# Graph attention on one core: the addition of x goes from VectorE to GpSimd

## What is computed

```python
h = jnp.maximum(_layernorm(x, axis=-1), 0.0)
# inside _L0_gnn_ref, with h as its x
    h = jnp.einsum('ni,hif->hnf', x, W)
    s1 = jnp.einsum('hnf,hf->hn', h, a1)
    s2 = jnp.einsum('hnf,hf->hn', h, a2)
    scores = jax.nn.leaky_relu(s1[:, :, None] + s2[:, None, :], negative_slope=0.2)
    scores = jnp.where(adj[None] > 0, scores, NEG_BIG)
    att = jax.nn.softmax(scores, axis=-1)
    out = jnp.einsum('hnm,hmf->hnf', att, h)
    return jax.nn.elu(out)          # heads side by side, 512 wide
x = x + _L0_gnn_ref(h, adj, W, a1, a2)
```

## Time and profile before

| what | value |
|---|---|
| median of three runs | 812.9 us |
| the profiled execution's own time | 814.42 us |
| its span in the trace | 812.6 us |
| mean granted TensorE clock | 0.864 |
| DVE busy | 687.4 us, 85% of the span |
| PE busy | 610.1 us, 75% |
| ACT busy | 471.6 us, 58% |
| POOL busy | 388.6 us, 48% |

### The profile page before, as it was taken

One profiled execution on the slowest core, in us unless ns is written; L12 is line 12 of the kernel. 1 busy time (PEld: TensorE's weight loads), 2 busy tenths in 40 slices (PEclk: granted clock), 3 DMA queues, 4 the chain that ended last, 5 costly groups with the idle time before them and its releaser, 6 DMA issues.

```text
span 812.6 us, 9242 instructions
## 1 busy us (share of the span) xinstructions
PE 610.1 (75%) x2182; PEld 357.3 (44%) x2182; DVE 687.4 (85%) x2066; ACT 471.6 (58%) x695; POOL 388.6 (48%) x775
## 2 busy tenths in 40 slices
PE   0698988897688758553886697768878859988874
PEld 0364554454354434342543354444444435554442
DVE  4897998997777677564999799999999988999995
ACT  0647999989999989225565365647453213233322
POOL 4644544442333332227776336447375655757610
PEclk9998999989998997855999698886887869999997
DMA  9956999999999999328999999999996766969852
GB/s 289 424 207 229 339 411 417 417 403 407 422 421 419 420 421 423 150 66 316 407 409 417 406 367 400 413 414 397 410 398 199 263 194 204 297 206 296 288 174 105
DMA packets 65130, 269.51 MB, mean 332 GB/s; under 512 B 12145, under 2 KB 12145, under 8 KB 52786
## 3 DMA queue, kind: packets, MB, share of 16 engines
q1 hardware_dynamic: 45314, 203.12, 63.1%
q0 software_dynamic: 19760, 65.78, 23.6%
HBM read 243.49 MB, written 25.37 MB: 331 GB/s over the span
## 4 chain that ended last, share of the span: by engine, by line
DVE 26%; PE 12%; issue 8%; DMA 6%; POOL 3%; ACT 0%; DVEq 0%; POOLq 0%
DVE nodes L1098 8%; PE psO L1237 7%; DMA nodes<-table,list_column 4%; DVE places L248 4%; PE psO L1243 3%; DVE best L237 3%; DVE agg L1109 2%; DMA nodes<-table,column 2%; POOL nodes L934 2%; DVE to_row L1068 1%; DVE result L1121 1%; POOL nodes L929 1%; PE psC L1223 1%; DVE owner L1032 1%; PE psD L1238 1%
## 5 line engine op out<-in xcount | busy, mean ns | idle before, releaser
L601 PE MATMUL psH<-sb_W,normedT 128*128 128x512 f32 x384 | 225.5, 678 | 0.0
L1237 PE MATMUL psO<-nodes,ident 128*128 128x512 f32 x276 | 183.7, 758 | 43.5 <-issue 39.9
L227 ACT ACTIVATE packed<-adj_rows,eight 128x3072 uint8<-128x3072 int32 x66 | 188.3, 2853 | 0.7
L929 POOL DMA_INDIRECT nodes<-table,column x138 | 135.3, 980 | 85.5 <-PE psD L1244 45.0
L934 POOL DMA_INDIRECT nodes<-table,list_column x109 | 112.5, 1032 | 86.9 <-DVE list_column L1057 56.4
L1098 DVE TENSOR_TENSOR nodes<-nodes,psW 128x2048 f32<-128x2048 f32 (+4 forms) x66 | 138.7, 2142 | 0.0
L1243 PE MATMUL psO<-nodes,to_row 128*128 128x512 f32 x218 | 124.9, 661 | 6.3 <-DVE nodes L1098 6.1
L643 POOL TENSOR_TENSOR sb_node_sum<-sb_node_sum,h_rows 128x512 f32<-128x512 f32 x48 | 61.2, 1275 | 141.6 <-ACT h_rows L566 141.6
L602 PEld LDWEIGHTS psS<-sb_Wa,normedT 128*128 128x128 f32 x384 | 78.6, 205 | 103.5 <-issue 103.5
L248 DVE FIND_INDEX8 places<-best,packed 128x8 uint32<-128x96 f32 (+6 forms) x240 | 109.9, 465 | 0.0
L237 DVE MAX8 best<-packed 128x8 f32<-128x96 f32 (+6 forms) x240 | 102.8, 460 | 0.5 <-ACT packed L227 0.5
(11 more groups left out here) (177 smaller groups left out, 923.3 us busy)
## 6 DMA issues: line engine op xcount, KB each, us to landing
adj_rows<-in_adj_dram SPq DMA_DIRECT2D x66, 1536.0 KB, 10.7
sb_adj_rows<-in_adj_dram SPq DMA_DIRECT2D x30, 1536.0 KB, 14.6
table<-h_rows SPq DMA_DIRECT2D x48, 260.0 KB, 9.0
sb_x_rows<-in_x_dram SPq DMA_DIRECT2D x48, 256.0 KB, 9.2
kept<-in_x_dram SPq DMA_DIRECT2D x19, 512.0 KB, 7.0
out_dram<-result SPq DMA_DIRECT2D x19, 512.0 KB, 4.0
kept<-in_x_dram SPq DMA_DIRECT2D x10, 256.0 KB, 8.8
out_dram<-result SPq DMA_DIRECT2D x10, 256.0 KB, 7.6
```

Source lines behind the costliest of these rows:

```text
L227: nc.scalar.activation(words.bitcast(mybir.dt.uint8), sb["adj_rows"][buffer_of(i)][:], ACT.Square, bias=sb["eight"][:], scale=-17.0, accum ...
L601: nc.tensor.matmul(psH[:, t % 2], normedT[:, t % 2, kc], sb["W"][:, kc], start=(kc == 0), stop=(kc == KC - 1))
L929: nc.gpsimd.indirect_dma_start(out=nodes[:, node_at[u] + i * w.direct + j], out_offset=None, in_=table, in_offset=bass.IndirectOffsetOnAxi ...
L1237: nc.tensor.matmul(psO[:, o, to], sb["ident"][:], nodes[:, n0 + q, 0:HF], start=a, stop=False)
```

## The change

The kernel before computes kept = max(agg, 0) + x on DVE in `normalise`, and result = (exp(min(agg, 0)) - 1) + kept on DVE in `finish`. The kernel after leaves the first away and computes result = max(exp(min(agg, 0)) - 1, agg) on DVE in `finish`, which is elu(agg), and then result = result + x on POOL, in place, in a new function `add_x`. POOL does this for the group of unit u-4 after it has issued all gathers of unit u, that is two units later than `finish` stands on DVE. The store and the next load of x, which SP issues, wait for POOL's addition.

```diff
+            def add_x(g):
+
+                w, o = GROUPED[g], g % 2
+                pool.wait_ge(bent, g + 1)
+                pool.wait_ge(x_loaded[o], 16 * (g // 2 + 1))
+                nc.gpsimd.tensor_tensor(result[:, o, 0:w.tiles], result[:, o, 0:w.tiles], kept[:, o, 0:w.tiles], ALU.add).then_inc(finished, 1)
             for u, w in enumerate(UNITS):
...
                                                  ).then_inc(gathered[k], 16)
+                if u >= 4 and UNITS[u - 4].last:
+                    add_x(UNITS[u - 4].group)
+            for u in range(U - 4, U):
+                add_x(UNITS[u].group)
...
                 if g >= 2:
-                    dve.wait_ge(grown_done, g - 1)
+                    dve.wait_ge(bent, g - 1)
                 nc.vector.tensor_tensor(by_head(agg[:, o, 0:w.tiles]), by_head(psO[:, o, 0:w.tiles]),
...
-                dve.wait_ge(agg_done, g + 1)
-                dve.wait_ge(x_loaded[o], 16 * (g // 2 + 1))
-                nc.vector.scalar_tensor_tensor(kept[:, o, 0:w.tiles], agg[:, o, 0:w.tiles], 0.0, kept[:, o, 0:w.tiles],
-                                               ALU.max, ALU.add).then_inc(kept_done, 1)
 
             def finish(g):
                 w, o = GROUPED[g], g % 2
                 dve.wait_ge(grown_done, g + 1)
-                dve.wait_ge(kept_done, g + 1)
-                nc.vector.scalar_tensor_tensor(result[:, o, 0:w.tiles], result[:, o, 0:w.tiles], -1.0, kept[:, o, 0:w.tiles],
-                                               ALU.add, ALU.add).then_inc(finished, 1)
+                nc.vector.scalar_tensor_tensor(result[:, o, 0:w.tiles], result[:, o, 0:w.tiles], -1.0, agg[:, o, 0:w.tiles],
+                                               ALU.add, ALU.max).then_inc(bent, 1)
```

More of the change, by code:

```diff
@@ L880, in attend_edges @@
         below_done, agg_done, grown_done, finished = sem("below_done"), sem("agg_done"), sem("grown_done"), sem("finished")
-        recips, kept_done = sem("recips"), sem("kept_done")
+        recips, bent = sem("recips"), sem("bent")
         late_step, late_counted, late_placed, late_planned = sem("late_step"), sem("late_counted"), sem("late_placed"), sem("late_planned")
```

## The result

The changed kernel is slower: 819.03 us (median of 5 runs, 815.89 to 819.65) against 811.7 us for the kernel before on the same chip, a ratio of 1.0079 with a 95% interval of 1.0049 to 1.0108. In a later comparison it took 817.0 us (12 runs) against 812.67 us, ratio 1.0061, interval 1.0042 to 1.0080. The forecast was 816.4 us. The profiled execution took 815.89 us with a span of 814.3 us; that is the lowest of its runs, so the 1.7 us between the two profiled spans (812.6 and 814.3) understate the change.

What follows compares the result with a forecast made beforehand. DVE bounded the kernel before; additions would overfill POOL's late queue. Last gather and tile 38's addition to 788.05, plus 2.2, 29.4 and 2.45, less 6.0 gained, gave 816.1 us; 0.3 more for the median, 816.4. Range 804.5 to 821.5.

Steps and rivals of the forecast that it cites:

- The 12.5 free microseconds: POOL's last 64 gathers before the change: gathers and gaps occupy 86.4 of 98.90 us, leaving some 12.5 us free.
- exclusion weak: Rival: wide additions let DVE's two-input instructions through, about 806 us; chance 0.22, shared with a cheap addition.
- DVE stays the bound: Rival: DVE still sets the pace, 26.6 us go and 2.45 are added at the end, 788.8 us; chance 0.05.
- The gain ahead of the late tiles: Before 663.5 us: 11.8 us of removed DVE work less 5.8 us of losses, 6.0 us gained.
- The term for the hold: Before 663.5 us, additions hold DVE: 1.8 and 1.5 us at `turn`, 1.0 for tile 10, 0.5 for smaller touches.
- small touches: Before 663.5 us: minor holds of DVE by additions, put at 0.5 us.
- The late gathers: Before 663.5 us: gathers landing late in the full DMA queues, put at 1.0 us.
- POOL's stretch: From tile 28's first gather to POOL's last: 84.4 us gathers, 22.0 additions, 2.3 waits, together 108.7 us.
- the 86.4: POOL's time for its last 64 gathers before the change: 67.48 us busy plus 18.9 us of gaps.
- The tail: Behind the last gather: 2.45 us addition, 2.2 to `weigh`, 29.4 to the end, 2.45 for the last group's addition.

Runs made afterwards that it cites:

- `no_add`: Changed kernel with x loaded but added nowhere, SP storing behind DVE's finish; 791.11 us, ratio 0.9732 to the kernel before, in its second run.
- the second pair: Profiles of the unedited changed kernel and the unedited kernel before, run again together in a later comparison; ratios 1.0061 and 0.9999 to the kernel before.

## Why the prediction was right, and where its sizes were off

**The mechanism was right in the main; one step failed in kind, and luck in the sizes hid it.** Wide additions take 2.36 us. POOL has no wait over 0.65 us between the gathers of tiles 28 and 46. `turn` is stretched at tiles 14 and 16. From one addition to the next the units of 6 blocks take 9.8 to 11.1 us and that of 8 blocks 13.1, as named. The 12.5 free microseconds were POOL's, and they were used up. The rival "exclusion weak" would have needed 806 us, and the instructions that end just behind an addition, which it rules out, are there. Behind tile 28, though, it is `turn` that most additions stretch; of the front and score instructions that the prediction named, only front is stretched, at two additions (680.97 and 693.26). "DVE stays the bound" (788.8 us) is close to what `no_add` took (791.1): it holds only with no addition at all.

**The gain ahead of the late tiles was mis-sized.** Forecast 6.0 us at the first gather of tile 28. Measured from the first score: 293.9 after against 298.4 before, 293.2 against 295.7 in the second pair, so 4.5 and 2.5 us. With no addition it is 286.6 us, 9.1 to 11.8 us better than before, so the removed work was priced about right at 11.8, and the additions cost 6.6 to 7.3 us of it instead of the forecast 5.8. The term for the hold was the wrong one: 1.8 us at tile 14, 1.5 at tile 16, 1.5 for tile 10 and small touches. Measured is 2.69 + 1.25 at the two `turn`s, 0.36 at tile 10's (576.43, 1.05 us), and 1.78 and 1.56 at two places that the working did not name, in the edge search of the next rows: L305 at 547.25 (2.05 us for 0.27) and L293 at 561.28 (1.83 for 0.27). The first of these:

```profile
547.25 2.05 DVE L305 SCALAR_TENSOR_TENSOR cands<-best,falling 128x128 f32<-128x128 uint8 x1
```

```profile
547.85 1.28 POOL L925 TENSOR_TENSOR result<-result,kept 128x512 f32<-128x512 f32 x1
```

That is 7.6 us for the 4.8; in the second profile of the changed kernel it is 6.5, with `turn` at tile 14 held for 1.6 us instead of 2.7. An addition holds any instruction with two SBUF inputs that comes by, and not `turn` alone. The late gathers were put at 1.0; behind the first score DVE waits once for a gather, 7.1 us where it was 4.9 (7.0 and 2.7 in the second pair).

**POOL's stretch was too dear.** Forecast 108.7 us for the 64 gathers and 9 additions, measured 103.9. The additions took 21.3 us instead of 22.0, and the waits 1.3 instead of 2.3. The gaps were 17.4 us instead of the 18.9 inside the 86.4, since where an addition stands its two gaps (0.01 and 0.16) replace one of 0.30, and two more are counted in the waits; and fewer gathers were slow beside DVE, 63.9 us busy for the 65.5. Together 4.8 us, so +5.2 us instead of +10.0. No row of before shows an addition between two gathers; the 0.10 us that I added for the step were a guess, and it went the other way.

**The tail was too cheap.** Forecast 36.5 us from the end of the last gather, measured 39.8. Score of tile 44 starts 778.54 - 774.52 = 4.0 us behind it instead of 2.45, because the addition holds `turn` (775.58, 1.62 us) with `agg` still to come. `weigh` follows 3.44 us after score, not 2.18. This is the step that failed in kind: I took only the last group's `kept` as lying beside ACT. In all of the last four, `agg` to `finish` takes 3.44 us with `kept` in it or without, since Relu and Exp set it: 780.84 - 777.40 in the changed kernel, and before:

```profile
778.64 1.22 DVE L1109 TENSOR_TENSOR agg<-psO,recip 128x1024 f32<-128x1024 f32 x1
...
782.08 1.23 DVE L1121 SCALAR_TENSOR_TENSOR result<-result,kept 128x1024 f32<-128x1024 f32 x1 [0.21 <-ACT result L991]
```

In `finish` DVE waits for ACT 8.1 us in all, against 2.6. So four of the 29 removed instructions, not one, were worth nothing; with no addition at all the tail is as long as before (36.8 us).

Gain, POOL's stretch and tail are -4.5 + 5.2 + 2.8 = +3.5 us (437.6 - 434.2 = 3.4, first pair of profiles, from the first score on) against the forecast's -6.0 + 10.0 - 0.5 = +3.5. The second pair gives -2.5 + 5.0 + 2.8 = +5.3 us. That the errors cancel is luck; the forecast time was nearer than its terms. By the medians the kernel is 7.3 us slower in the first comparison and 4.3 in the second (ratios that make 6.4 and 5.0 us), where 3.5 was forecast. The profiled execution of the changed kernel was the fastest of its five, so the first pair of profiles does not show all of that, and the rest of it is in no term found here.

## What to carry to other kernels

Work moved to POOL costs at least twice: its time in POOL's queue, wherever that queue is nearly full (count the gaps between gathers, not the busy share), and the time for which DVE instructions with two SBUF inputs stand still. The second is avoided by placing the POOL instruction beside DVE work that reads PSUM, or beside MAX8 and FIND_INDEX8 (no run here has an addition beside a TENSOR_SCALAR out of SBUF); the first only by not moving the work in that stage. So such a move is decided stage by stage: here half of it, put in the right place, is 1.0% faster than the old kernel, all of it in that place 0.3% faster, and all of it where the change has it 0.6 to 0.8% slower. A DVE share of 97% after a change is no sign that DVE is the bound: look for instructions longer than their twins.

## What the runs showed of the hardware

- A DVE instruction with two SBUF inputs that starts up to 0.6 us ahead of the addition's recorded start is still held to its end (547.25 against 547.85; 693.26 against 693.85). It ends 0.03 us (`slot`, own time 0.15, 683.15 against 683.12) to 0.56 us (`turn`, own time 0.69) behind the recorded end, so the hold ends an estimated 0.12 us ahead of it, from these two. The Trainium skill says that GpSimd's recorded spans are not to be trusted ("Perfetto Trace Analysis", section "GPSIMD Engine Instruction"); these rows agree. L305 at 547.25, with 0.27 us of its own, should have been done at 547.52, so I read the recorded start as at least 0.3 us late, which no run here shows by itself.
- A POOL memset holds a DVE TENSOR_SCALAR with its one input and its output in SBUF (`list_column`, 0.17 us: 1.24 us, and 2.3 us in the last units; `owner` once 2.79 us for 0.35). It holds none with two inputs, nor TENSOR_REDUCE, MAX8 or FIND_INDEX8; an addition holds those with two inputs. Beside an addition, MAX8, FIND_INDEX8, and instructions with an input from PSUM keep their time.
- Adding a buffer to itself takes 1.90 us for 1024 elements where two buffers take 2.36, and 1.05 for 1.28 us at 512.
- Two profiles of one kernel differed by 2.2 us from the first score to the end, and one chip was 2% slower for the kernel before than in the other three comparisons. So ratios are each to the kernel before in the same comparison; where two of different comparisons are set side by side above, a chip's own part in the difference is not ruled out.
